# A transformer block on one Trainium2 core: the decision on the bound moved to the tail, single stores for the last tiles, and seven unread products on TensorE

## The reference

```python
x = x + attention(layernorm(x))      # 16 heads of 16, causal softmax, output projection
x = x + ffn(layernorm(x))

def ffn(x):
    base = x @ W.T + b
    logits = x @ gate_w.T + gate_b                    # 8 experts
    topk_logits, topk_idx = jax.lax.top_k(logits, 2)
    gates = softmax(topk_logits)
    xA = einsum('nd,erd->ner', x, lora_A)             # rank 16
    delta_all = einsum('ner,eor->neo', xA, lora_B)
    return base + sum(gates * delta_all at topk_idx)
```

## Time and profile before

| | |
|---|---|
| median of 3 runs | 330.92 us (333.09, 330.9, 330.92) |
| profiled execution, whole | 332.83 us |
| its span, first to last instruction | 330.9 us |
| mean granted TensorE clock | 0.987 |
| PE busy | 314.3 us, 95% |
| ACT busy | 273.9 us, 83% |
| DVE busy | 190.2 us, 57% |
| POOL busy | 72.6 us, 22% |

### The profile page before, as it was taken

One profiled execution on the slowest core, in us unless ns is written; L12 is line 12 of the kernel. 1 busy time (PEld: TensorE's weight loads), 2 busy tenths in 40 slices (PEclk: granted clock), 3 DMA queues, 4 the chain that ended last, 5 costly groups with the idle time before them and its releaser, 6 DMA issues.

```text
span 330.9 us, 8638 instructions
## 1 busy us (share of the span) xinstructions
PE 314.3 (95%) x3478; PEld 119.1 (36%) x3478; DVE 190.2 (57%) x613; ACT 273.9 (83%) x306; POOL 72.6 (22%) x99
## 2 busy tenths in 40 slices
PE   7999989999999999999999999997999999999794
PEld 2453434434434343334432333232223323322272
DVE  5627796576667627466164773583566456611752
ACT  2377799998999999999999999996899999999110
POOL 6377102222221302213021311130220322100000
PEclk9999999999999999999999999997999999999978
DMA  6567684101172102000139000000000000000001
GB/s 202 164 171 214 201 217 112 34 2 34 30 195 66 35 3 50 2 16 12 23 73 232 2 18 18 0 18 1 18 3 16 18 2 16 19 18 1 2 2 66
DMA packets 18986, 19.23 MB, mean 58 GB/s; under 512 B 10368, under 2 KB 15744, under 8 KB 18944
## 3 DMA queue, kind: packets, MB, share of 16 engines
q1 hardware_dynamic: 18848, 18.52, 21.0%
q10 hardware_dynamic: 96, 0.13, 0.2%
HBM read 12.35 MB, written 6.29 MB: 56 GB/s over the span
## 4 chain that ended last, share of the span: by engine, by line
PE 73%; ACT 10%; issue 6%; DVE 4%; DMA 3%; SPq 2%; POOL 0%; ACTq 0%
PE acc L940 28%; PE aux L768 18%; PE scores L923 17%; ACT probs L1067 10%; PE scores L768 4%; DMA x_sb<-x 2%; PE aux L810 1%; DMA k_stack<-k_dram 1%; DVE probs L1276 1%; PE aux L761 1%; DMA q_dram<-q_stack 1%; PE aux L823 1%; PE scores L855 1%; PE aux L868 1%; SPq L545 1%
## 5 line engine op out<-in xcount | busy, mean ns | idle before, releaser
L1067 ACT ACTIVATE probs<-scores 128x1024 f32<-128x1024 f32 x272 | 257.4, 1030 | 21.2 <-PE scores L923 19.5
L940 PE MATMUL acc<-probs,v_aug 128*32 128x512 f32 (+3 forms) x1280 | 136.5, 534 | 2.3 <-DVE turned L1282 1.6
L923 PE MATMUL scores<-q_stack,k_stack 64*128 64x512 f16 (+3 forms) x640 | 80.0, 350 | 4.8 <-ACT probs L1067 3.1
L1276 DVE TENSOR_TENSOR probs<-probs,mask_sb 128x512 f32<-128x512 f32 (+1 forms) x80 | 51.7, 677 | 26.6 <-ACT probs L1067 26.5
L923 PEld LDWEIGHTS scores<-q_stack,k_stack 64*128 64x128 f16 x640 | 22.9, 94 | 97.6 <-ACT probs L1067 82.0
L940 PEld LDWEIGHTS acc<-probs,v_aug 128*32 128x32 f32 x1280 | 37.0, 109 | 50.6 <-issue 31.9
L1580 POOL TENSOR_TENSOR rstd<-ve,minus_half 128x1 f32<-128x1 f32 x12 | 7.1, 589 | 69.1 <-DVE ve L1311 69.1
L1585 POOL TENSOR_TENSOR exp_gap<-euler,top_gap 128x1 f32<-128x1 f32 x12 | 7.4, 613 | 57.5 <-DVE top_gap L1337 53.0
L1327 DVE COPY ffn<-aux 128x392 f32<-128x392 f32 x12 | 6.8, 564 | 22.3 <-PE aux L768 22.3
L768 PE MATMUL aux<-wffn_sb,yT 128*32 128x392 f32 x192 | 18.3, 498 | 0.0
L1282 DVE STREAM_TRANSPOSE turned<-acc 128x512 f32<-128x512 f32 (+1 forms) x17 | 11.6, 680 | 9.8 <-PE acc L940 9.8
(11 more groups left out here) (163 smaller groups left out, 286.3 us busy)
## 6 DMA issues: line engine op xcount, KB each, us to landing
q_stack<-q_dram SPq DMA_DIRECT2D x14, 256.0 KB, 4.0
k_stack<-k_dram SPq DMA_DIRECT2D x28, 128.0 KB, 3.8
x_sb<-x SPq DMA_DIRECT2D x3, 512.0 KB, 5.6
out<-ffn SPq DMA_DIRECT2D x12, 128.0 KB, 1.7
q_dram<-parts SPq DMA_DIRECT2D x16, 64.0 KB, 2.2
k_dram<-parts SPq DMA_DIRECT2D x8, 128.0 KB, 2.2
wqkv_sb<-wqkv SPq DMA_DIRECT2D x3, 256.0 KB, 4.2
x_sb<-x SPq DMA_DIRECT2D x2, 256.0 KB, 3.1
```

The costliest lines, as they stand in the source:

```text
L923: m = pe.matmul(scores[bank_of(u)][:, j, col:col + n], k_stack[row:row + STACK, kb // TPC, 2 * i + p, kb % TPC * P:(kb % TPC + 1) * P], q_ ...
L940: m = pe.matmul(acc[32 * hp:32 * hp + 32, lo:CHUNK], v_aug[:, kb, QUAD * i + hp, :], probs[:, u % PROBS, hp % 2, col:col + CHUNK - lo], st ...
L1067: act.activation(probs[:, u % PROBS], scores[bank_of(u)][:], ACT.Exp, scale=EXP_SCALE).then_inc(exp_done, 1)
L1276: dve.tensor_tensor(tile, tile, mask, ALU.min).then_inc(causal_done, 1)
```

## The change

`decide_bound` is no longer called behind the last `read_norms`, but in the tail, on DVE, between the last normalise and the first top two. Seven products of `q_stack` values into `acc` are issued on PE between the last o and the first turn of y, behind a wait for the last transpose of `acc`; nobody reads them. `last_finish` adds the bias to the first pair at once and to the tiles 2 and 3 one by one. The first pair is stored by SP, tile 2 by ACT's queue and tile 3 by SP; the counts that wait for these stores go from two to three.

```diff
+WARM_LAST = 7
...
             def general():
-                sp.wait_ge(last_result_out, 16 * 2)
+                sp.wait_ge(last_result_out, 16 * 3)
...
-            for p in range(2):
-                sp.wait_ge(last_result_ready, p + 1)
-                at = TILES - TPC + 2 * p
-                sp.dma_start(out[at:at + 2].rearrange("n p d -> p n d"), last_result[:, pair_of(p), :]
-                             ).then_inc(last_result_out, 16)
+            sp.wait_ge(last_result_ready, 1)
+            at = TILES - TPC
+            sp.dma_start(out[at:at + 2].rearrange("n p d -> p n d"), last_result[:, 0:2, :]).then_inc(last_result_out, 16)
+            sp.wait_ge(last_result_ready, 3)
+            sp.dma_start(out[TILES - 1], last_result[:, 3, :]).then_inc(last_result_out, 16)
...
-            sp.wait_ge(last_result_out, 16 * 2)
+            sp.wait_ge(last_result_out, 16 * 3)
...
             last_o(0)
             last_o(1)
+
+            pe.wait_ge(acc_read, TURNS)
+            for _ in range(WARM_LAST):
+                pe.matmul(acc[:], q_stack[:, 0, 0, 0:P], q_stack[:, 0, 0, :], start=True, stop=True)
             last_turn_y(0)
...
+            act.wait_ge(last_result_ready, 2)
+            act.dma_start(out[TILES - 2], last_result[:, 2, :]).then_inc(last_result_out, 16)
...
                 dve.tensor_reduce(norms[:, c:c + 1], aux[0:64], AX_X, ALU.max).then_inc(norm_read, 1)
-                if c == NCHUNK - 1:
-                    decide_bound()
...
-            def last_finish(p):
-                dve.wait_ge(last_out_psum, p + 1)
-                dve.tensor_tensor(last_result[:, pair_of(p), :], y_banks[p].rearrange("p (n d) -> p n d", n=2),
-                                  biases_sb[:, 0:D].unsqueeze(1).to_broadcast([P, 2, D]), ALU.add
+            def last_finish(tiles, pairs):
+                dve.wait_ge(last_out_psum, pairs)
+                n, at = tiles.stop - tiles.start, tiles.start % 2
+                bank_of_pair = y_banks[tiles.start // 2].rearrange("p (n d) -> p n d", n=2)
+                dve.tensor_tensor(last_result[:, tiles, :], bank_of_pair[:, at:at + n, :],
+                                  biases_sb[:, 0:D].unsqueeze(1).to_broadcast([P, n, D]), ALU.add
                                   ).then_inc(last_result_ready, 1)
...
             for t in range(TPC):
                 last_normalise(t)
+
+            decide_bound()
             for p in range(2):
                 last_top_two(p)
             last_gates_of_all()
-            for p in range(2):
-                last_finish(p)
+            last_finish(slice(0, 2), 1)
+            for t in (2, 3):
+                last_finish(slice(t, t + 1), 2)
```

## The result

| | before | after |
|---|---|---|
| median of 4 runs each | 331.11 us | 328.07 us |
| lowest and highest | 330.9, 333.09 | 327.88, 328.41 |
| profiled execution, whole | 332.83 us | 328.41 us |
| its span | 330.9 us | 326.6 us |
| mean granted clock of it | 0.987 | 0.997 |

The ratio of the runs is 0.9911, with a 95% interval of 0.9881 to 0.994: 0.9% faster. That is inside the forecast's range of 325.0 to 329.3, but outside the likeliest case's own range (325.3 to 327.0), and within the 1% that the forecast called "same", to which it gave 0.34 against 0.62 for "faster". The likeliest time, 326.1, was 2.0 us too low. The span of the profiled execution was foretold as 326.1 and is 326.6.

What follows compares the result with a forecast made beforehand. PE was taken to bound the kernel (95% busy), except where its values waited for DVE's decision and in the tail. Terms 1.46 + 1.55 + 0 + 1.4 + 0 + 0.4 = 4.8 us gave 326.1 us, range 325.0 to 329.3.

Steps and rivals of the forecast that it cites:

- the likeliest case: Whole kernel: all terms hold, median 326.1 us, own range 325.3 to 327.0; chance 0.50.
- The decision leaves its place: Behind the reduce of the norms: without the decision ahead, the transpose of acc starts earlier; 1.46 us off.
- The clock behind it: PE work behind the norms: with the hole nearly closed the clock stays up; 1.55 us more off.
- Seven products at nothing: PE's hole between last o and first turn: products take 1.7 to 1.9 us, fit inside; 0, at worst 0.9 late.
- The clock in the tail: Turns and ranks on PE: full clock instead of half takes 1.4 us off, bounds 1.2 to 1.7.
- The decision in its new place: DVE's wait between last normalise and first top two: 1.46 us fits; cost 0, at worst 0.2.
- The stores: End of kernel: three stores in place of two gain 0.4 us, bounds -0.2 to 0.9.
- The sum on the profiled execution: Whole kernel: all terms together take 4.8 us off the profiled execution, 332.83 to 328.0 us.
- Rival 1: Both holes: fast runs never had the low clock, so only 1.46 and 0.4 come off, 329.1 us; chance 0.27.
- The sign named beforehand: Kernel before: the forecast is wrong if its runs at 330.9 us have a clock of 1.00.
- The slower rival: Tail: clock low when the products start, turns 0.9 us late, 332.1 us in all; chance 0.04.
- Rival 2: One of the two half-clock stretches stays or comes elsewhere, costing about 1.5 us: 327.6 us; chance 0.14.

Runs made afterwards that it cites:

- experiment 10: Changed kernel with the last pair added at once and stored by one 256 KB DMA from ACT's queue; median 328.29 us, ratio 0.9907.
- experiment 5: Changed kernel run once more with no edit; median 328.4 us, ratio 0.9917.
- experiment 11: Changed kernel with 14 unread products in place of 7; median 329.01 us, ratio 0.9927.
- experiment 9: Changed kernel with the two single stores exchanged, tile 2 by SP and the last tile 3 by ACT; median 328.42 us.
- experiments 3: Kernel before with only the seven products added; median 330.5 us, ratio 0.9979.
- 6: Changed kernel without the seven products; median 329.25 us, ratio 0.9934.
- 7: Changed kernel with the decision back at its old place behind the reduce of the norms; median 331.15 us, ratio 0.9992.
- 12: Changed kernel with the decision in its old step, directly behind the transpose of acc instead of in the tail; median 328.32 us, ratio 0.9908.

## Why the prediction was right or wrong

Distances between instructions compare the profiles free of where the early steps came to lie:

| kernel | clock low behind the norms | reduce to statistics | clock low in the tail | statistics to last pair's add |
|---|---|---|---|---|
| before | yes | 88.92 us | yes | 14.45 us |
| before, run again | no | 87.33 | yes | 14.54 |
| only the decision moved | no | 85.83 | yes | 14.78 |
| only the stores | yes | 88.97 | yes | 14.19 |
| products only | no | 87.33 | no | 13.17 |
| change without move | yes | 88.99 | no | 13.17 |
| change without products | no | 85.82 | yes | 14.17 |
| change | no | 85.82 | no | 13.17 |

*The decision leaves its place: right.* 87.33 - 85.82 = 1.51 us, foretold as 1.46.

*The clock behind it: right in size where it falls.* 88.92 - 87.33 = 1.6, foretold as 1.55; the two other profiles with the fall have 1.6 and 1.7. ACT hid nothing.

*Seven products at nothing: right.* They took 1.69 us against 1.7 and ended ahead of the turn.

*The clock in the tail: right for the profiled execution.* 14.45 - 13.17 = 1.28, foretold as 1.4 within 1.2 to 1.7. Over the five profiles with the fall it is 1.00 to 1.61, wider than the bounds. It grows with how late the low stretch comes against the first turn: 0.15 us behind its start in the change without products (1.00), 0.2 in the stores alone (1.02), 0.7 and 0.9 in before (1.28 and 1.37), 1.6 in the decision alone (1.61). The earlier it comes, the more of it lies over turns that wait for DVE anyhow.

*The decision in its new place: right,* with 0.25 of idle time left behind it.

*The stores: right in size on average* (0.34 against 0.4), with the cause open. Single tiles landed 2.2 to 3.3 us after issue, not near 1.7. The prediction's size effect is there in part: the last tile landed 2.8 to 3.3 after issue (3.0 on average in the seven profiles), the slower of two pairs from SP 3.2 to 3.6 (3.4 in the five). But a pair from ACT's queue took 2.6 (experiment 10), which size doesn't explain. Nor does the length of the issue alone. SP's second issue took 0.94 in the earlier trace rows, and 0.84 to 1.32 in the others but for one of 0.33 (experiment 5), ACT's 0.39 to 0.44 each time. Yet with the 0.33 it is 4.40 from the add to the end, more than the 4.16 behind an issue of 1.21 (experiment 11), and ACT's short issue of the last tile in experiment 9 gained nothing. On the rule of the Trainium skill that was weighed ("DMA: Bandwidth & Descriptors", "Issuing engines are not separate DMA queues": more issuing engines save issue time alone) these runs don't decide.

*The sum on the profiled execution: right.* 4.8 foretold; 4.3 measured on the spans, and 4.9 with the 0.64 by which the early steps came later in the second profile.

*The step that failed* is the one behind the sum: "If that is the recording's price or a constant, the same 4.8 comes off the median". It is neither. What lies around the span is 1.93 in one profile, 1.8 in the other and 1.7 to 1.95 in the 83 executions; the six of before between 330.83 and 330.96 had spans of 329.0 to 329.2. The profiled execution had both low stretches, and only 26 of 83 do. So the two terms for the clock, 2.95 together, may be counted only by the share of executions in which the clock falls. Rival 1 had the mechanism and gave it 0.27. It took an all or nothing: 329.1 would hold if no execution of before had a low stretch. By the groups, those without one go from 330.17 to 328.31, 1.86 less, which is rival 1's 1.46 + 0.4 (that the hundredths agree is luck, as the executions of a group scatter by more than 1 us); those with both go from 332.53 to 328.31, 4.2 less. The median lies between, and 3.0 is what came out. Counted by the share of stretches that fell, (2 x 26 + 36) of 166 or 0.53, the 2.95 become 1.56, and 1.86 + 1.56 = 3.4 off the median is 327.7. The measured time lies in the stated range only because that range was stretched to rival 1's 329.1. The sign named beforehand, a clock of 1.00 in runs of before at 330.9, didn't come so: those have 0.992 or 0.993, one low stretch, and the executions with none are the faster ones.

Two things stay open. The groups differ by 2.36 us (332.53 - 330.17), while the traces give 1.6 + 1.28 = 2.9 for the two stretches. The kept profiles point to why: of the five with the hole at the norms, the three in which the clock fell start the reduce at 222.89 to 223.06, the two in which it didn't at 223.54 and 223.98, so the executions with the fall may begin this part sooner and lose less in all. Five profiles don't prove it. And the half clock itself could not be forced. That it follows the holes is shown by what closing or filling them does: in the tail it is there in five of five profiles with the hole and in none of nine without, at the norms in three of five and in none of nine, and the counts of executions go the same way (experiments 3, 6, 7 and 12).

The slower rival, low clock when the products start, was in none of the profiles. Rival 2, a stretch that stays or comes elsewhere, holds in one of ten executions by its mean clock, without a trace of it.

## What to carry to other kernels

Before a profile's sum is taken off a median, look at the mean granted clock of each execution: a term that rests on a fall of the clock counts only by the share of executions in which it falls. An instruction that nobody waits for must not stand ahead of the one that frees a bank for TensorE; here the same 1.5 us of VectorE's work cost 1.5 to 3.1 us ahead of it and nothing behind it. A hole on TensorE that can't be closed can be filled with unread products, as long as they end before the hole does.

## What was not expected of the hardware

A hole of 1.63 us on TensorE was followed by 1.2 GHz in some executions of one and the same program and not in others (of 83, by their mean clock, 26 had two low stretches, 36 one and 21 none, counting the tail's hole of 1.82 us too). Between the groups with none and with two lie 2.36 us of the 4.2 over which the kernel before spreads (329.3 to 333.5). And a second store issued by SyncE within a microsecond of the first held its queue for 0.84 to 1.32 us in all profiles but one, in place of 0.38, while one from ScalarE's queue at that time took 0.39 to 0.44. The time to the end did not follow this length.
